# Unread 512-column matrix products on TensorE in the last and first bodies of a fused attention kernel

## What is computed

```python
x = x + 0.5 * _L0_ffn_ref(_layernorm(x), router_w, router_b, expert_w, expert_b)
x = x + _L0_attn_ref(_layernorm(x), Wq, Wk, Wv, Wo, lq1, lq2, lk1, lk2, rms_w)
x = x + 0.5 * _L0_ffn_ref(_layernorm(x), router_w, router_b, expert_w, expert_b)
```

## Time and profile before

| what | us |
|---|---|
| device time, median of 3 runs | 1736.35 |
| the three runs | 1735.72, 1736.35, 1740.88 |
| device time of the profiled execution | 1733.46 |
| span in its profile, first to last instruction | 1730.9 |
| mean granted TensorE clock over the span | 0.889 |
| PE busy / DVE busy / ACT busy / POOL busy | 1420.5 / 1450.0 / 1249.1 / 1066.3 |

### The profile page before, as it was taken

The page is one execution under the profiler, slowest core; times in us unless marked ns, Lnnn a source line. Parts: engine busy times, 40 slices in busy tenths (PEclk is TensorE's granted clock), DMA queues, the critical chain, the costliest instruction groups (busy, mean ns, idle before and its releaser), DMA issues. The chain is left out here.

```text
span 1730.9 us, 45556 instructions
## 1 busy us (share of the span) xinstructions
PE 1420.5 (82%) x10646; PEld 993.6 (57%) x10688; DVE 1450.0 (84%) x5825; ACT 1249.1 (72%) x3426; POOL 1066.3 (62%) x1493
## 2 busy tenths in 40 slices
PE   3998465888899999999999999999999988886710
PEld 3543232666666666666666666666666666665300
DVE  6868536888899999999999999999999788773387
ACT  2354245888788989999999899999998677774320
POOL 5412354665678787788878778878887555554100
PEclk9999686888899999999999999999999666676955
DMA  8012423111112112211122211222111100001196
GB/s 323 2 51 83 159 63 64 33 33 33 33 45 54 49 49 59 53 47 47 47 54 55 54 51 49 54 54 53 47 47 49 36 18 18 18 18 37 49 347 245
DMA packets 166282, 116.00 MB, mean 67 GB/s; under 512 B 122577, under 2 KB 126801, under 8 KB 166226
## 3 DMA queue, kind: packets, MB, share of 16 engines
q1 hardware_dynamic: 166226, 115.33, 22.8%
HBM read 50.26 MB, written 33.55 MB: 48 GB/s over the span
## 5 line engine op out<-in xcount | busy, mean ns | idle before, releaser
L1229 DVE TENSOR_SCALAR_CACHE_REDUCE bank<-bank,nesc 128x512 f32<-128x512 f32 (+3 forms) x1024 | 508.8, 553 | 74.3 <-PE bank L1965 73.1
L1706 ACT ACTIVATE ex<-bank,nbias 128x512 f32<-128x512 f32 (+3 forms) x1024 | 542.9, 549 | 36.9 <-DVE bank L1229 36.7
L1994 PEld LDWEIGHTS bank<-vs,pr 128*128 128x128 f32 x2560 | 337.9, 208 | 52.2 <-DVE att L1277 24.2
L1994 PE MATMUL bank<-vs,pr 128*128 (+1 forms) x2560 | 355.5, 290 | 13.4 <-DVE att L1277 13.3
L1723 ACT ACTIVATE pr<-bank 128x128 f32<-128x128 f32 (+3 forms) x512 | 233.3, 456 | 141.0 <-PE bank L1977 140.6
L1963 PE MATMUL bank<-ks,hall 96*128 (+2 forms) x1024 | 283.9, 322 | 37.8 <-DMA hall<-hall 21.7
L1549 POOL TENSOR_SCALAR ex<-ex,gam 128x128 f32<-128x128 f32 (+3 forms) x512 | 307.9, 612 | 0.0
L1977 PE MATMUL bank<-cst,df 128*128 128x128 f32 x1280 | 253.1, 299 | 54.2 <-ACT pr L1723 51.5
L1256 DVE CUSTOM_DVE_ANT_0 df<-ex 128x128 f32<-128x128 f32 (+3 forms) x512 | 267.2, 540 | 3.8 <-PE bank L1977 2.5
L1706 ACT ACTIVATION_READ_ACCUMULATOR ex<-bank,nbias 128x1 f32 x1024 | 234.4, 229 | 0.0
L1965 PE MATMUL bank<-mask_b,ident_b 128*128 128x128 bf16 x1024 | 218.5, 232 | 0.0
(11 more groups left out here) (357 smaller groups left out, 2913.5 us busy)
## 6 DMA issues: line engine op xcount, KB each, us to landing
hall<-turned SPq DMA_DIRECT2D x336, 64.0 KB, 2.1
x_dram<-hall SPq DMA_DIRECT2D x8, 1024.0 KB, 4.9
hall<-x_dram SPq DMA_DIRECT2D x8, 1024.0 KB, 14.8
c_y<-y_dram SPq DMA_DIRECT2D x8, 1024.0 KB, 14.4
out_dram<-hall SPq DMA_DIRECT2D x8, 1024.0 KB, 4.7
hall<-in_x SPq DMA_DIRECT2D x7, 1024.0 KB, 13.6
x<-x_dram SPq DMA_DIRECT2D x28, 256.0 KB, 2.6
x_dram<-x SPq DMA_DIRECT2D x28, 256.0 KB, 2.7
```

What stands on the lines that cost most here:

```text
L1229: dve.tensor_scalar(part, part, nesc[:, 0:1], None, ALU.mult, ALU.min, accum_out=nbias[:, j, i, a:a + 1]).then_inc(bias_done.sem, 1)
L1706: ac.activation(ex[j % 4][:, a, lo:hi], energy(j, i)[:, a, :], ACT.Exp, bias=nbias[:, j, i, a:a + 1], scale=-1.0, accum_out=esum[:, j, i, ...
L1994: mm = pe.matmul(bank[:, 7, t * DV:(t + 1) * DV], pr[j % 2][:, lo + k * P:lo + (k + 1) * P], val, start=(k == 0), stop=(k == t))
```

## The change

Matrix products are added on PE whose result nobody reads. `idle(n)` adds n products of the 128x128 identity with a slice of the expert weights (float16, 512 columns), which write bank 4 (late) or bank 5 (first bodies). With `late=True` they are issued where tau is None: in bodies 27 to 31 at slots 2, 5, 8, 11, 14, 17, 20 and 23, and in body 32 at slots 2, 5, 8 and 11. Ahead of each such group PE waits until ACT has emptied bank 4 for the last time. With `late=False` they are issued where pi is None: in bodies 0 to 4 at slots 3, 13, 18 and 21. n is 4 everywhere. In all other bodies nothing is issued.

```diff
+                def idle(n, late=True):
+
+                    def f(tau, pi):
+                        if (tau if late else pi) is None:
+                            if late:
+                                turned_out.wait(pe, 3 * NT - 1)
+                            for i in range(n):
+                                pe.matmul(bank[:, 4 if late else 5, :], ident_h[:, :], we_h[:, i % KT, :], start=True, stop=True)
+                    return f
+
...
-                           {1: [prep(turn_x)], 4: [prep(project(0, 0))], 6: [prep(project(0, 1))],
-                            8: [post(turn_heads), prep(project(1, 0))], 10: [prep(project(1, 1))],
-                            11: [post(product_o(0)), post(product_o(1))], 12: [prep(turn_chunks(0))],
-                            15: [prep(project(2, 0))], 16: [prep(project(2, 1))], 18: [post(turn_x2)],
-                            19: [post(route), prep(turn_chunks(1))], 22: [post(expert(0)), post(expert(1))],
-                            23: [prep(turn_chunks(2))]},
+                           {1: [prep(turn_x)], 2: [idle(4)], 3: [idle(4, False)], 4: [prep(project(0, 0))],
+                            5: [idle(4)], 6: [prep(project(0, 1))],
+                            8: [idle(4), post(turn_heads), prep(project(1, 0))], 10: [prep(project(1, 1))],
+                            11: [idle(4), post(product_o(0)), post(product_o(1))], 12: [prep(turn_chunks(0))],
+                            13: [idle(4, False)], 14: [idle(4)], 15: [prep(project(2, 0))],
+                            16: [prep(project(2, 1))], 17: [idle(4)], 18: [idle(4, False), post(turn_x2)],
+                            19: [post(route), prep(turn_chunks(1))], 20: [idle(4)], 21: [idle(4, False)],
+                            22: [post(expert(0)), post(expert(1))], 23: [idle(4), prep(turn_chunks(2))]},
```

## The result

| | before | changed |
|---|---|---|
| median of 4 runs, us | 1738.09 | 1714.47 |
| lowest and highest, us | 1735.72, 1740.88 | 1708.26, 1718.20 |
| profiled execution, us (span) | 1733.46 (1730.9) | 1708.26 (1705.9) |
| mean granted clock | 0.889 | 0.929 |

The account below looks back on a forecast made before the run. DVE bounds middle bodies, PE at half speed the late ones. Gains of 31.5 (late), 3 (body 32) and 4 us (early), 38.5 in all, take 1733.46 to 1695; with 2.9 us for the median, 1698 us, range 1676 to 1730.

Parts of the forecast that it names:

- the late gain: Bodies 27 to 31: groups keep the clock up, bodies 27 to 30 take 37.6 us; 31.5 us won, bounds 15 to 38.
- What bounds the late bodies: Bodies 27 to 31: PE at half speed bounds them now; with the clock up DVE does, at 36.3 us a body.
- I take two such falls and a little for late energies, 1.3 us: Late bodies: two short clock falls, 0.5 us each as in a middle body, plus late energies, added to 36.3 us.
- So the group is mostly hidden: Late bodies: groups sit where PE waits for ACT; where not hidden, energies come up to 0.86 us late.
- The place of the fall: Late bodies: steps of 4.5 us leave up to 3.7 us of attention alone between two groups, where the clock may fall.
- The rule on idle gaps: Skill page's rule that idle gaps between bursts of products lose the clock; by it 1773 us, set aside for the trace.
- The added wait and body 32: Wait for ACT to empty bank 4: nothing, or up to 0.9 us once; body 32: 3 us won, between -3 and 6.
- The early part: Bodies 0 to 5: clock still falls but rises earlier; 0.8 us a body, 4 us in all, bounds -6 to +16.
- (a): Rival: the early bodies' clock clears too, 16 us there and 54 us in all, total 1682 us; chance 0.22.
- (b): Rival: the late clock is won half, 15 us late and 2 for the rest, total 1719 us; chance 0.13.
- (c): Rival: the clock pattern stays and groups lengthen the bodies, 37 us slower in all, total 1773 us; chance 0.10.
- (d): Rival: nothing happens, as unread products are dropped or DVE's 36.3 us isn't reached; total 1736 us, chance 0.03.

Follow-up runs that it names:

- late_narrow: Changed kernel with its late groups alone, each product 16 columns wide in place of 512; 1741.8 us, ratio 1.0006 to the kernel before.
- plug: Changed kernel plus one group of four in step 2 of each late body, before weigh(0), where PE waits for DVE's copy; 1703.7 us, ratio 0.9809.
- late_turned: Changed kernel with its late groups alone, each group's four products replaced by sixteen 128-column transposes; 1713.9 us, ratio 0.9875 to the kernel before.
- early_23: Changed kernel with the early group of slot 21 moved to slot 23, behind the turned chunks; 1704.6 us, ratio 0.9801 to the kernel before.
- late_n8: Changed kernel with its late groups alone, eight products in each instead of four; 1725.9 us, ratio 0.9921 to the kernel before.
- thin: The kernel of plug without the late groups at slots 11 and 23; 1691.3 us, ratio 0.9728 to the kernel before.
- late_only: Changed kernel without the early groups of bodies 0 to 4, late groups kept; 1716.8 us, ratio 0.9869 to the kernel before.
- early_only: Changed kernel without the late groups, early groups kept; 1734.2 us, ratio 0.9974 to the kernel before.
- thin_no_plug: Changed kernel without the late groups at slots 11 and 23, and no group added before weigh(0); 1698.4 us, ratio 0.9768 to the kernel before.

## Why the prediction was right, and where it was not

The mechanism was right, wide products where PE had narrow work raise the clock, and the total fell inside the range. The range was wide enough for that: 25 of 38.5 us came, and what is missing is missing from one term, the late gain.

**What bounds the late bodies.** Right. With the clock at 1.00 and no group in DVE's way a late body takes 36.45 to 36.49 us, where DVE's busy time and a middle body's idleness had given 36.3. And late_narrow shows that it is the array work that moved the clock.

**The late gain, 31.5 us.** Measured 17.3, so this is the term that was mis-sized, by two steps. "I take two such falls and a little for late energies, 1.3 us" took the price of a fall from a middle body, 0.5 us for 3.4 us at the low clock. In a late body 3.4 us at the low clock cost 1.4 to 1.7 us, three times as much, and the one fall of bodies 28 to 31 is twice as long, 6.8 us: together 3.1 us a body, by plug. What follows it is narrow work at half speed, which may be why it is long; no run shows that. The second step is "So the group is mostly hidden". It is, for the groups in front of PE's wait for ACT. But the two beside `product_o` and `expert` stood in a queue that was already 2.6 to 2.8 us long (12 or 13 products at 0.215 us), with DVE at its end: 1.4 us a body. In all 36.5 + 1.4 + 3.1 = 41.0, the measured body. The signs named for a right late step were 36.5 to 38.5 us and about 1 us of DVE's wait for energies; bodies 28 to 30 have 41.0 and 4.1, and only the clock over 0.9 came.

**The place of the fall.** I had looked for stretches without wide products, and judged all steps alike, 4.5 us long with 3.7 us between two groups. The trace of before had the wait for att only as 0.8 us in body 29, since PE was late itself. Once PE was quick, the same wait became 2.5 us. I should have asked what PE would wait for next when it is not the bound any more.

**The rule on idle gaps.** The Trainium skill, page "TensorE: Matmul & The Clock Gate", section "HAM oscillation — how this bites in real kernels", ascribes the loss of clock to idle gaps, and the prediction set it aside. That was right for the kernel before, where PE was busy 39.12 of 44.16 us at 0.69, and its consequence, 1773 us, did not come. It was too quick for the kernel after: the one fall that remained came at the end of the longest gap of the body, 2.54 us. That plug, which fills this gap, removes or shortens the fall goes the way of the rule; that late_turned's body 29 has the same gap and no fall shows that a gap of this length alone doesn't decide.

**The added wait and body 32.** Body 27 needed no more than 39.36 us and shows no cost of the wait. Body 32 took 47.5 us, where about 47 was named as the sign, and with what follows it won 2.0 us of the 3 forecast.

**The early part, 4 us.** Measured 4.9 us in bodies 0 to 5, and 4 to 5 alone. The reasons held in body 2: it still has its fall, 6.8 us instead of 10.2, and takes 40.27 us, 0.8 less, as the text had it. The others don't follow it: body 0 won 1.5 us, body 1 lost 1.2, bodies 3, 4 and 5 won 2.4, 0.9 and 0.5. That the sum comes so near is in part luck. That the group of slot 21 stands ahead of the wrong 6 us is shown by early_23, which moved it.

**The rivals.** (a), a clear early clock, did not come, but is mostly reached by moving one group: bodies 0 to 5 take 229.0 us in early_23 and 239.5 before. (b) has the time, 15 us from the late bodies and 1719 in all, but not the mechanism: the late clock was not won half. In bodies 28 to 30 it rose from 0.69 to 0.92, and the time at the low clock fell from 27 us to 6.8. (c) is excluded by the changed kernel's faster time and its late clock of 0.92; even late_n8, with twice the products, is faster than before. (d) is excluded by the 32 records of L1953 in a late body and by thin's bodies of 36.5 us.

## What to carry to other kernels

Where PE is slow because its clock is down, and not because it has much to do, unread products can pay: 1.5% of the whole kernel as the change places them, and 3% in the best placement tried. What counts is where they stand: here a place right in front of a wait of PE's that no other dense work covered paid, and places beside the two blocks of wide products that DVE was waiting for cost their own time. After such a change look for the next wait in a new trace, because the wait that decides is hidden while PE is late.

## What the runs showed that I had not expected

Groups of transposes hold the clock as well as groups of 512-column products of equal length do (1713.9 us for late_turned and 1716.8 for late_only). Twice the products cost less than their own time against late_only: 64 a body instead of 32 lengthened bodies 28 to 30 by 0.2 to 1.9 us, since the time at the low clock fell from 6.8 us to 3.4 or none; at full clock the price shows, 41.4 us against 37.9. And the changed kernel's runs scatter by up to 0.6% (1708.3 to 1718.2). A possible reason, not tested, is that a body that ends a little earlier or later meets the next weak stretch at another point of the clock's course: body 26, without any edit, took 40.2 us in the changed kernel, 44.5 us in early_only and thin_no_plug, and 43.0 us in thin.
